# Four instead of two trees fetched by row, with sums kept in PSUM and a new order of all engines

## The reference

```python
query = unit_projection(x @ Wq.T + bq)      # keys, values alike
out = unbind(cumsum(bind(keys, values)), query)
x = x + out
...
logits = x @ W_in.T + b_in
acts = silu(logits)                          # dmap: 1 on the path of the token
out = (acts * dmap).reshape(B, WIDTH) @ W_out.T
```

## Time and profile before

| | us |
|---|---|
| median of 3 runs | 1904.74 |
| profiled execution, whole | 1902.03 |
| its span, first to last instruction | 1899.9 |
| TensorE busy | 1846.0 (97%) |
| VectorE busy | 1548.9 (82%) |
| ScalarE busy | 1117.4 (59%) |
| GpSimd busy | 943.0 (50%) |

### The profile page before, as it was taken

The page is one execution under the profiler, slowest core; times in us unless marked ns, Lnnn a source line. Parts: engine busy times, 40 slices in busy tenths (PEclk is TensorE's granted clock), DMA queues, the critical chain, the costliest instruction groups (busy, mean ns, idle before and its releaser), DMA issues.

```text
span 1899.9 us, 40007 instructions
## 1 busy us (share of the span) xinstructions
PE 1846.0 (97%) x14488; PEld 1389.5 (73%) x14488; DVE 1548.9 (82%) x2938; ACT 1117.4 (59%) x2151; POOL 943.0 (50%) x737
## 2 busy tenths in 40 slices
PE   8499999999999999999999999999999999999978
PEld 6478777778777778877777877777877777787755
DVE  4888888888888888888888888888888888888783
ACT  5666565566565556656556656556655555665643
POOL 1254445564445565444556445556544556545450
PEclk9799999999999999999999999999999999999999
DMA  8032232222133222223222213322223322222312
GB/s 288 12 87 79 68 100 92 74 88 88 55 100 100 70 85 88 73 82 100 79 87 87 85 59 100 98 68 88 88 59 96 100 77 77 88 69 86 89 56 67
DMA packets 181785, 163.18 MB, mean 86 GB/s; under 512 B 140161, under 2 KB 140801, under 8 KB 181761
## 3 DMA queue, kind: packets, MB, share of 16 engines
q1 hardware_dynamic: 163328, 95.48, 17.0%
q0 software_dynamic: 18432, 67.38, 10.7%
HBM read 95.72 MB, written 16.78 MB: 59 GB/s over the span
## 4 chain that ended last, share of the span: by engine, by line
PE 90%; DVE 2%; DMA 1%; ACT 1%; issue 0%; SPq 0%; DVEq 0%; ACTq 0%
PE bank_l L532 31%; PE bank_l L589 30%; PE bank_p L482 23%; PE bank_l L542 3%; PE bank_i L482 2%; DMA arena<-xn_pair 1%; PE bank_i L553 1%; PE bank_i L560 0%; SPq L341 0%; DVE xn_pair L1126 0%; DVE arena L1239 0%; ACT xn_pair L721 0%; ACT arena L794 0%; PE bank_i L559 0%; DVE arena L1249 0%
## 5 line engine op out<-in xcount | busy, mean ns | idle before, releaser
L532 PE MATMUL bank_l<-arena,win_mem 128*128 128x256 f16 x5376 | 625.1, 273 | 16.5 <-DMA arena<-xn_pair 16.5
L589 PE MATMUL bank_l<-wout_mem,arena 128*128 128x512 f16 x2688 | 593.4, 379 | 0.0
L532 PEld LDWEIGHTS bank_l<-arena,win_mem 128*128 128x128 f16 x5376 | 525.0, 98 | 80.5 <-DMA arena<-xn_pair 15.1
L482 PE MATMUL bank_p<-arena,wf_hi 128*128 128x256 f16 x3072 | 505.8, 273 | 2.7 <-ACT arena L740 2.7
L589 PEld LDWEIGHTS bank_l<-wout_mem,arena 128*128 128x128 f16 x2688 | 260.6, 98 | 308.8 <-DVE arena L1226 11.7
L482 PE MATMUL bank_p<-arena,wf_lo 128*128 128x256 f16 x1536 | 419.0, 273 | 0.0
L985 POOL TENSOR_TENSOR arena<-arena 128x512 f32<-128x512 f32 x96 | 121.8, 1269 | 553.1 <-ACT arena L749 553.1
L482 PEld LDWEIGHTS bank_p<-arena,wf_hi 128*128 128x128 f16 x3072 | 299.6, 98 | 37.6 <-ACT arena L740 3.0
L1226 DVE SCALAR_TENSOR_TENSOR arena<-arena,s_act 128x512 f16<-128x512 f32 (+1 forms) x256 | 238.7, 942 | 80.4 <-ACT arena L804 66.3
L794 ACT ACTIVATE arena<-bank_l,bias_in,s_logit 128x256 f32<-128x256 f32 x448 | 229.2, 554 | 121.4 <-PE bank_l L542 121.0
L1219 DVE TENSOR_SCALAR dec<-bank_l,thr,off 128x256 bf16<-128x256 f32 x256 | 136.0, 542 | 92.5 <-PE bank_l L532 91.0
(11 more groups left out here) (175 smaller groups left out, 2500.6 us busy)
## 6 DMA issues: line engine op xcount, KB each, us to landing
arena<-in_x SPq DMA_DIRECT2D x32, 512.0 KB, 3.5
arena<-arena SPq DMA_DIRECT2D x32, 512.0 KB, 2.9
out<-arena SPq DMA_DIRECT2D x64, 256.0 KB, 2.1
wout_mem<-in_w_in_t SPq DMA_DIRECT2D x1, 3584.0 KB, 16.1
arena<-in_w_out_t SPq DMA_DIRECT2D x1, 3584.0 KB, 13.8
arena<-xn_pair SPq DMA_TRANSPOSE x128, 2.8
arena<-in_leaf_rows,leaf_row POOLq DMA_INDIRECT x128, 5.7
win_mem<-in_wq SPq DMA_DIRECT2D x1, 1024.0 KB, 7.5
```

The lines of the kernel that those rows point to most:

```text
L482: mm = pe.matmul(bank, a, b, start=(n == 0), stop=(n == len(pairs) - 1))
L532: mm = pe.matmul(bank_l[t % 4][:, c * T:(c + 1) * T], a[:, k, w:w + P], x2t[:, :, b, k, :], start=(c == 0 and k == 0 and m == 0), stop=((t ...
L589: mm = pe.matmul(bank_l[j][:, :], a[:, m, tok], w[:, m, :], start=(m == 0 and a is a_hi and w is wout_hi), stop=(m == DENSE - 1 and a is a ...
```

## The change

GATHERED holds trees 0 to 3, fetched in two rounds: trees 0 and 1, then 2 and 3. 12 dense columns remain (two leaf columns fewer in the input and output weights). The activations of a tree stay in its PSUM bank: Silu writes in place, and the high and low parts are read from there, so a bank is free for tree t + 4 after the low part instead of after Silu. xn2 is written to bank_i, and ScalarE copies it to SBUF (`keep_row`) for the row products. The leaf sums run in PSUM, in bank_l[2 + j], which ScalarE starts with a copy of x1 (`begin_total`); the additions of block i and its results are made by VectorE in step i + 1. The one-column products move from bank_i to bank_p. K and V are projected before Q. The down products are split: trees 0 to 5 for both halves, then trees 6 and 7, with the counts of tree 7 between. SyncE's transposes of xn2 stand behind those of the next xn1. The prologue works through K, V, Q and moves a part of the preparation of the feed-forward weights into step 0.

In the two long orders (ScalarE's and VectorE's step) the removed lines are left out, as the listing above shows the old order, and so is what only step 0 does.

```diff
-GATHERED = (0, 1)
+GATHERED = (0, 1, 2, 3)
...
-ROUNDS = ((0, 1),)
+ROUNDS = ((0, 1), (2, 3))
...
-HELD = 3
+HELD = 4
...
-Q, K, V, G_IN, G_OUT = range(5)
+K, V, Q, G_IN, G_OUT = range(5)
...
+        xn2 = [bank_i[j][:, :] for j in range(J)]
+        total = [bank_l[2 + j][:, :] for j in range(J)]
+        sp_rows = bank_p[1][:, 0:3 * J].rearrange("p (j q) -> p j q", q=3)
+        sp_sums = bank_p[1][:, 8:8 + J + 1]
+        sp_size = bank_p[1][:, 16:16 + 3 * J].rearrange("p (j q) -> p j q", q=3)
...
-                for j, have in enumerate((first, second)):
-                    sp.wait_ge(consts_done, 1)
-                    if not isinstance(i, int) or i:
-
-                        sp.wait_ge(logit_full, classified)
-                    sp.wait_ge(xn2_lo_ready, have)
-                    if isinstance(i, int) and i == 0:
-
-                        sp.wait_ge(wout_hi_done, 1)
-                        sp.wait_ge(wout_lo_done, 1)
-                    transpose(j, x2t, x2t_ready)
-                if nxt:
                     for j in range(J):
                         sp.wait_ge(consts_done, 1)
                         sp.wait_ge(proj_full, projected)
                         sp.wait_ge(xn1_lo_ready, split1[j])
                         transpose(j, xt, xt_ready)
-                for j, have in enumerate((first, second)):
+                if attn:
+                    for j in range(J):
+                        sp.wait_ge(consts_done, 1)
+                        sp.wait_ge(logit_full, classified)
+                        sp.wait_ge(xn2_lo_ready, split2[j])
+                        transpose(j, x2t, x2t_ready)
+                for j in range(J):
                     sp.wait_ge(consts_done, 1)
-                    sp.wait_ge(y_ready, have)
+                    sp.wait_ge(y_ready, results[j])
                     sp.dma_start(out_v[i][:, j, :], y[:, j, :]).then_inc(y_stored, 16)
...
+                    pe.wait_ge(a_lo_ready, TREES * i + t - 3)
...
-                        pe.wait_ge(act_ready, TREES * (i - 1) + 5 + t)
+                        pe.wait_ge(leaf_added, LEAVES * i)
...
-            def down(i, j):
+            def down(i, j, trees):
                 tok = slice(j * P, (j + 1) * P)
-                if isinstance(i, int) and i == 0:
+                if isinstance(i, int) and i == 0 and trees[0] == 0:
                     pe.wait_ge(wout_hi_done, PIECES)
                     pe.wait_ge(wout_lo_done, PIECES)
-                pe.wait_ge(act_ready, TREES * i + 5 + j)
-                for t in range(TREES):
+                if trees[0] == 0:
+                    pe.wait_ge(a_lo_ready, TREES * i + 5 + j)
+                for t in trees:
                     if j == 0:
-                        if t == 3:
-                            counts(i, TREES - 1)
                         pe.wait_ge(a_lo_ready, TREES * i + t + 1)
                     for m in [COLUMN[t, c] for c in range(2) if (t, c) in COLUMN]:
                         for a, w in ((a_hi, wout_hi), (a_hi, wout_lo), (a_lo, wout_hi)):
                             mm = pe.matmul(bank_l[j][:, :], a[:, m, tok], w[:, m, :],
                                            start=(m == 0 and a is a_hi and w is wout_hi),
                                            stop=(m == DENSE - 1 and a is a_lo))
-                mm.then_inc(out_full, 1)
+                if trees[-1] == TREES - 1:
+                    mm.then_inc(out_full, 1)
...
+                pe.wait_ge(x2t_ready, 16 * J * (i + 1))
+                pe.wait_ge(xn2_kept, J * (i + 1))
...
-                    project(n, Q)
                     project(n, K)
                     project(n, V)
+                if isinstance(i, int) and i == 0:
+                    peaks_in_row(G_OUT)
+                if attn:
+                    project(n, Q)
+                if isinstance(i, int) and i == 0:
+                    peak_to_all(G_OUT)
                 logits(i, 0, 0)
                 logits(i, 1, 0)
+                if attn:
+                    nyquist_rows(n)
                 counts(i, 0)
                 logits(i, 2, 0)
-                logits(i, 2, 1)
+                counts(i, 1)
                 logits(i, 3, 0)
-                logits(i, 3, 1)
-                counts(i, 1)
+                counts(i, 2)
                 logits(i, 4, 0)
+                counts(i, 3)
                 leaf_rows_of(i, 0)
-                if attn:
-                    nyquist_rows(n)
                 logits(i, 4, 1)
                 logits(i, 5, 0)
-                counts(i, 2)
+                counts(i, 4)
+                logits(i, 6, 0)
                 logits(i, 5, 1)
-                counts(i, 3)
-                logits(i, 6, 0)
                 logits(i, 6, 1)
-                if attn:
-                    nyquist_sums(n)
-                counts(i, 4)
+                leaf_rows_of(i, 1)
                 counts(i, 5)
                 logits(i, 7, 0)
+                if attn:
+                    nyquist_sums(n)
                 logits(i, 7, 1)
                 counts(i, 6)
-                down(i, 0)
-                down(i, 1)
+                down(i, 0, range(0, 6))
+                counts(i, TREES - 1)
+                down(i, 1, range(0, 6))
+                down(i, 0, range(6, TREES))
+                down(i, 1, range(6, TREES))
                 if attn:
                     transform_back(i)
...
+            def high2(n, j):
+                act.wait_ge(ln2_done, J * n + j + 1)
+                act.activation(xn_pair[:, j, 0, :], xn2[j], ACT.Copy).then_inc(xn2_hi_ready, 1)
+            def keep_row(n, j):
+                if not isinstance(n, int) or n:
+                    act.wait_ge(leaf_dot_ready, LEAVES * n)
+                act.wait_ge(xn2_lo_ready, J * n + j + 1)
+                act.activation(kept[:, j, :], xn2[j], ACT.Copy).then_inc(xn2_kept, 1)
+            def begin_total(i, j):
+                act.wait_ge(a_lo_ready, TREES * i + 7 + j)
+                act.activation(total[j], x1[:, j, :], ACT.Copy).then_inc(total_begun, 1)
...
-                if t >= HELD:
-                    act.wait_ge(a_lo_ready, TREES * i + t + 1 - HELD)
-                elif not isinstance(i, int) or i:
-                    act.wait_ge(a_lo_ready, TREES * i)
                 for c in [c for c in range(2) if (t, c) in COLUMN]:
-                    ins = act.activation(acts[:, t % HELD, c * T:(c + 1) * T], bank_l[t % 4][:, c * T:(c + 1) * T],
+                    ins = act.activation(bank_l[t % 4][:, c * T:(c + 1) * T], bank_l[t % 4][:, c * T:(c + 1) * T],
                                          ACT.Silu, bias=bias_in[:, c, t:t + 1], scale=s_logit[:, 0:1])
...
+                odd_copy(i, 0)
                 act.activation(root_warm[:, :], ln_eps[:, :], ACT.Sqrt)
+                odd_copy(i, 1)
+                if attn:
+                    evac_re(n, K)
+                    evac_im(n, K)
+                    square(n, K)
+                std(i, mv2, rs2, ln2_mv, ln2_std)
+                if attn:
+                    evac_re(n, V)
+                    act.wait_ge(xt_ready, 16 * J * (n + 1))
+                high2(i, 0)
+                if attn:
+                    root(n, K)
+                    evac_im(n, V)
+                    square(n, V)
+                high2(i, 1)
                 if attn:
                     evac_re(n, Q)
+                    root(n, V)
                     evac_im(n, Q)
                     square(n, Q)
+                keep_row(i, 0)
+                if attn:
+                    root(n, Q)
+                leaf(i, 0)
...
+                silu(i, 0)
...
+                act_high(i, 0)
...
+                keep_row(i, 1)
+                if attn:
+                    nyquist_size(n)
+                leaf(i, 1)
+                silu(i, 1)
+                act_high(i, 1)
+                silu(i, 2)
...
+                leaf(i, 2)
+                leaf(i, 3)
+                act_high(i, 2)
+                leaf_row_copy(i, 0)
+                silu(i, 3)
                 if nxt:
                     std(n + 1, mv1, rs1, ln1_mv, ln1_std)
                 act_high(i, 3)
                 silu(i, 4)
                 if nxt:
                     shifted(n + 1)
+                leaf_row_copy(i, 1)
+                if nxt:
+                    act.wait_ge(x2t_ready, 16 * J * (i + 1))
+                    high(n + 1, xn1, ln1_done, xn1_hi_ready)
+                act_high(i, 4)
                 silu(i, 5)
                 act_high(i, 5)
                 silu(i, 6)
                 act_high(i, 6)
                 silu(i, 7)
                 leaf_silu(i, 0)
                 leaf_silu(i, 1)
+                begin_total(i, 0)
+                leaf_silu(i, 2)
+                act_high(i, 7)
+                begin_total(i, 1)
+                if attn:
+                    z_high(n)
+                leaf_silu(i, 3)
...
+                    sum_squares(n, K)
+                    add_eps(n, K)
+                    sum_squares(n, V)
```

(83 more changed lines are left out.)

386 lines of the change are left out of this document (177 added, 209 removed).

## The result

The change makes the kernel slower: 2095.03 us (median of 4 runs, 2090.15 to 2110.52) against 1904.38 for the kernel before on the same chip. The ratio is 1.1015, 95% interval 1.0984 to 1.1046. I had predicted 1857.

The account below looks back on a forecast made before the run. TensorE's stream bounds the 56.31 us step; two columns fewer give a 51.2 floor, 3.6 of lateness makes 54.9, 0.3 of small waits 55.2. With prologue and ends, 146 + 31 T gives 1857 us, range 1789 to 1907.

Parts of the forecast that it names:

- The step that failed: Tree 2's rows land at 43.3 us, counted from TensorE starting K's projections; VectorE's next low part due at 48.4.
- the 0.15 for a slower kernel: Whole kernel: chance 0.15 of slower; reasons named were GpSimd's chain, dearer table loads and VectorE's used-up slack.
- The third: Rival: GpSimd's chain behind the fetches becomes the bound, step 57.3 us, 1922 us in all; chance 0.14.
- The last remark: VectorE's queue named as the likeliest error: one wait of it moves everything behind; no size given.
- The hole before the first logits: TensorE, second layer norm: transposed rows land at 17.3 us, logits due at 15.7, late by 1.6 us.
- Before tree 4's logits and tree 3's counts: TensorE waits for VectorE's chain to decision 3: ready at 27.0, due at 23.4; 3.6 us late, including the 1.6.
- GpSimd: slack: GpSimd's last low part ends at 52.6, contended 53.2; transform back due at 53.5; slack 0.3 to 0.9 us.
- Table loads: ScalarE: two Silu and two root table loads a step, 2.6 us, without hurting TensorE; dearer loads had chance 0.02.
- the free value: VectorE's low parts with one PSUM input beside GpSimd: 0.73 us taken, not the contended mean of 1.10.
- First transform: End of prologue: VectorE has 22 us left from 56, so near 78; 9.4 us off, bounds 4 and 14.
- Step 0: First step gets moved prologue work back: 60 us before, the new step plus 6 now.
- From the last transform to the end: Last step: unhidden layer norm (14.1 us), 1.4 more for moved additions, 5.2 saved by columns; 2.7 us less.

Follow-up runs that it names:

- Experiment 3: Changed kernel with SyncE's two transposes of the first layer norm waiting until all fetched rows have landed, nothing left out: 1866.06 us, ratio 0.9803.
- experiment 4: Changed kernel with the first layer norm's two transposes replaced, at the same place in SyncE's queue, by plain copies of the same bytes: 1896.24 us.
- experiment 7: Its table-load part: the kernel with transposes behind all rows, first layer norm's square root replaced by a linear function, two loads a step fewer: 1869.13 us.
- after: The changed kernel itself, with trees 0 to 3 fetched by row, against the kernel before: 2095.03 us, ratio 1.1015.
- experiment 6: Changed kernel's new order with only trees 0 and 1 by row (14 dense columns, four indirect DMAs a step): 2033.35 us, ratio 1.0682.
- experiments 3 and 5: The second: changed kernel with the first layer norm's transposes waiting only for rows of trees 0, 1 and 2: 1863.66 us, ratio 0.9787.

## Why the prediction was wrong

**The step that failed** is one sentence: "The DMAs land 5.7 us after issue: tree 2's rows at 43.3, which holds VectorE's queue for a moment, but its next low part is due only at 48.4." The rows came at 51.2 (1028.00 - 976.80), low part 6 at 52.4. The overlap of these fetches with SyncE's transposes stood at nothing in the sum; it costs 7.1 us a step. I took the landing from a kernel in which the fetches have the DMA engines nearly to themselves. I had walked through SyncE's queue for the transposes of the second layer norm and their neighbours, but never put the two transposes of the first one on the clock of the step: they are issued at 38.1 and 39.8 of it, among fetches issued at 37.4 to 42.1. Both numbers could be had: my own working had GpSimd's second round end at 40.5. Experiment 3 moves nothing but this and gives back 229 us; experiment 4 shows that it is mostly the transposes' form and not their bytes. Why a transpose costs the engines so much no run shows.

No rival had it; the 0.15 for a slower kernel stood on other reasons. The third was nearest in kind (a chain through the fetches becomes the bound), but it held that GpSimd's work would hold up the transform back. Its products and sums ended at 1027.7 (50.9 on the clock of the step, forecast 48.6), it then waited 5.89 us for z's high part, which stands on ScalarE behind the late low part, and its last product ended at 1036.15, ahead of the transform at 1036.91, which had no hole before it. The last remark, that one wait on VectorE moves everything behind it, was right.

**The rest of the schedule held.** With the collision taken out the step is 55.05 us (30 steps: 55.25) against 55.2 forecast. That it agrees so closely is in part luck: the stream is 51.8 against 51.2, 0.6 more, and the holes are 3.2 against 3.6, 0.4 less. In parts:
- The hole before the first logits: 1.6 forecast, 1.85 measured. Before tree 4's logits and tree 3's counts: 2.0 more forecast (3.6 in all), 0.85 + 0.54 measured.
- GpSimd: slack 0.3 to 0.9 forecast. In experiment 3 its last product ends at 1031.02 and the transform starts at 1031.12, with no hole. The slack is 0.1 us, below the forecast, and anything that delays it will be seen.
- Table loads: four a step as forecast, 1.28 us each; the two that experiment 7 takes out are hidden. The 2.66 us with drain of the Trainium skill (ScalarE: Activation LUTs, "What ACT_TABLE_LOAD costs") shows nowhere: the Silu starts 0.02 us behind its load.
- One PSUM input instead of two SBUF inputs: the free value, as taken. In experiment 3 both forms stand beside GpSimd's products (1021.88 to 1025.15):

```profile
1022.28 1.74 DVE L1329 SCALAR_TENSOR_TENSOR arena<-arena 128x512 f32<-128x512 f32 x1
...
1023.95 0.74 DVE L1315 SCALAR_TENSOR_TENSOR arena<-bank_l,s_act,arena 128x512 f16<-128x512 f32 x1
```

- Here the product with two SBUF inputs takes 1.74 us (0.68 free), the low part with one SBUF and one PSUM input 0.74. The rule in SBUF — State Buffer, "Who interferes with whom", of the Trainium skill is what this pair shows.
- First transform: near 78 forecast; 77.8 in experiment 3, 79.7 in after.

**Terms that were mis-sized** show in experiment 3, free of the collision. Step 0 takes 68.0 us where I had 61.2: besides the moved work itself, decisions and low parts behind it leave TensorE holes (2.49, 3.85 and 1.01 us among them). From the last transform to the end it is 60.5 us, not 56.3: the saving of two columns goes into the layer norm that nothing hides (TensorE waits 17.3 us for it, 14.1 before). Together 11 us, against the 9 by which experiment 3 (1866) misses 1857.

**Where the gain went.** Two columns fewer: -5.4 us a step. The order that they need: about +4 (experiment 6). Left is -1.2 a step and 10 us of prologue, less 8 at the ends: the 2% of experiments 3 and 5. The collision takes +7.1 a step on top.

## What to carry to other kernels

- When a change adds DMAs or moves their issue, put every transfer of the step on one clock, each with its queue, its kind and its window, and look for pairs that meet for the first time. A landing time read from the trace holds only for the neighbours that it had there.
- An instruction that waits for a DMA at the head of an engine's queue needs slack for the worst landing, not the median: here 7 us of delay in a fetch reached TensorE through one low part queued behind a product that was not urgent.
- Where two transfers collide, first try a wait that keeps them apart. It opened no hole here: the transposed rows, which land at 1028.8 in experiment 3, are due only at the projections at 1032.47.

## What the runs showed of the hardware

- DMA transposes and indirect fetches slow each other down when under way together: fetches 5.7 to 12.5 us (median from issue to landing), transposes 3.1 to 8.4 and 14.3 us, throughput from 251 to 304 down to 132 to 179 GB/s. A plain copy of the same bytes in the same place left the fetches at 6.2 us. The Trainium skill (DMA: Bandwidth & Descriptors, "Rules for kernel authors") says that a transpose next to ordinary DMAs needs nothing; here it needs its own time. The page speaks of safety there, the runs of time.
- Behind holes of 3.1 to 4.1 us TensorE's granted clock fell to 0.50 to 0.60 for some microseconds, and 24 down products took 7.04 in place of 5.34 us, 24 logits 5.30 in place of 2.79. So the 3.27 us hole cost 1.7 us more behind it. The length of the hole alone doesn't decide it: in after, the 24 down products behind a hole of 2.53 us at 957.65 took 7.03 us (granted clock 0.75), and those behind one of 2.52 us at 768.27 took 5.34 (1.00). Behind nearly all holes of 1.8 to 1.9 us before the first logits the clock stayed at 1.00 (24 logits in 2.79 us), but behind one of 1.95 us, at 220.12 in experiment 3, it fell to 0.66 and they took 4.46.
- A row product with two SBUF inputs beside GpSimd's products took up to 2.87 us (0.68 free), more than the 1.63 of the earlier trace rows.
